# Where the causal mask enters a row of scores, and in what order a pair of heads is worked

## The chip, the cores and the metric

One core of one Trainium2 chip runs the whole kernel. The metric is device time in microseconds of one execution, lower is better.

## The reference

Two sequences of 1024 tokens, width 256, pass through one layer, all in float32.

1. Layer norm of x; q, k, v for 16 heads of 128 (`einsum('ihd,bpd->biph')`); scores q·k; where a key comes after its query the score is replaced by -1e10; softmax of scores / sqrt(128); the weighted sum of v; the output projection W_O; the result is added to x.
2. Layer norm again, then a mixture of 32 experts (8 chosen for each token, by groups) plus a shared expert; the result is added.

The change touches step 1 alone.

## The kernel before

**The work of a pair.** Attention is done for 8 pairs of heads of sequence 0, then 8 of sequence 1: 16 pairs, p = 0 to 15. In the code `a` is the head within a pair, `c` the half of the queries (512 each), and k = 2a + c. Every float32 value is split into a high and a low part, and each product is three matmuls (`three`). A pair is a list of steps, named by kind, k and n:

- `Rk.n`: one row of scores, 128 queries against all keys up to their own: (r+1)·128 wide, r from 0 to 7, in `ps_s[r % 2]`. TensorE does the matmuls, VectorE the row maximum (L1237), ScalarE the exponential into `prob` (L1055). R0 is the rows r = 4 to 7 of head 0, R1 the rows 0 to 3 of head 1, R2 the rows 4 to 7 of head 1, R3 the rows 0 to 3 of head 0 of the next pair.
- `Tk.n`: up to four 128x128 transposes of `prob` into `ps_t` (L783, one bank of two), the high part copied by ScalarE to `pT_hi` (L1071), the low part by VectorE (L1252). There are three `pT` buffers, used in turn.
- `Vk.n`: the product of that transposed block with v, added up in `ps_z`. The last V of a k is followed by `z_hi` on ScalarE and `z_lo` on VectorE.
- `Wk.n`: half of the output projection, into a `ps_t` bank (T and W take the two banks in turn), then two adds to `acc` on VectorE (L1267).
- `X0` to `X11`: projections (q, k, then v) through the one bank `ps_x`: matmuls, a ScalarE copy of the high part, a VectorE subtraction for the low part.

**The order.** TensorE, ScalarE and VectorE each walk the same list in the same order, each doing its own share of every step, and each runs in order: a wait of one step holds all that stands behind it on that engine. `PAIR` serves pairs 0 to 6 and 11 to 14 as it stands, and pairs 9 and 10 with routing steps of VectorE woven in evenly (`SLOTS`, `DISPATCH`). Pairs 7, 8 and 15 have lists of their own (`MIDDLE`, `ROUTE`, `LAST`).

**The waits of the steps.**

- R (TensorE): the exponential of the row two before in the sequence of R steps, since `ps_s` has two buffers.
- T (TensorE): all four exponentials of its block, and VectorE's last read of its `ps_t` bank, that is, of the step two before it among the T and W steps.
- T (ScalarE): the V step of the block three before it, since that block lies in the same `pT` buffer:

```
act.wait_ge(s_bank, p * BANKED + m + 1)
act.wait_ge(s_pv, p * TRS + t + PV0 - 2)
```

Here t counts the T steps of the pair (T0.n is n, T1.n is 4 + n, T2.n is 12 + n, T3.n is 16 + n), V steps are counted in the same way, `PV0` is 3 and `TRS` is 24. So T step t waits for V step t - 3.

- V (TensorE): VectorE's low part of its T step. W: `z_lo`. X: VectorE's low part of the X step before.

Of the kernel before, what the change touches and what calls it, by code (L numbers as in the profile page):

```python
# [12 lines left out]
P = 128  # L13
# [20 lines left out]


PAIR = """
T0.0 T0.1 R0.0 X0 T0.2 V0.0 T0.3 V0.1 R0.1 X1 V0.2 V0.3 R0.2 R0.3 W0.0 W0.1 X2 T1.0 T1.1 R1.0
R1.1 X3 T1.2 V1.0 T1.3 R1.2 V1.1 T1.4 V1.2 V1.3 T1.5 R1.3 V1.4 T1.6 T1.7 X4 V1.5 T2.0 V1.6 T2.1
V1.7 X5 T2.2 R2.0 W1.0 R2.1 W1.1 V2.0 V2.1 V2.2 T2.3 X6 V2.3 R2.2 R2.3 W2.0 W2.1 X7 T3.0 T3.1
R3.0 R3.1 X8 V3.0 T3.2 V3.1 T3.3 X9 T3.4 V3.2 T3.5 V3.3 T3.6 V3.4 T3.7 R3.2 V3.5 V3.6 V3.7 X10  # L40
R3.3 W3.0 W3.1 X11
"""


# [201 lines left out]
def width(r):  # L246

    return P * (r + 1)
# [7 lines left out]
def build(nc, ctx, x, w_a, w_b, w_o, router, bias, experts, out):  # L256
    def sb(name, shape, dt=F32, until=ctx):
        return until.enter_context(nc.sbuf_tensor(name, shape, dt))
# [12 lines left out]
    ident, ident_bf = sb("ident", [P, P]), sb("ident_bf", [P, P], BF16)  # L271
    causal = sb("causal", [P, P], BF16)
# [46 lines left out]
    with ExitStack() as attention:  # L319
# [11 lines left out]
        k_lo = [sb(f"k_lo{a}", [P, S], F32R, attention) for a in range(2)]  # L331
# [71 lines left out]
    EXP0, BANK0, PV0, X0, O0 = 2, 2, 3, 1, 1  # L403
# [313 lines left out]
    def _(pe):  # L717
        pe.sem_inc(s_pv, PV0)
        pe.wait_ge(s_const, 8)

        def three(to, w_hi, w_lo, m_hi, m_lo, start, stop):

            pe.matmul(to, w_hi, m_hi, start=start, stop=False)  # L723
            pe.matmul(to, w_hi, m_lo, start=False, stop=False)  # L724
            return pe.matmul(to, w_lo, m_hi, start=False, stop=stop)  # L725

        def transpose_xn(q, d, bank):

# [6 lines left out]
        def project(b, n, bank, weights):  # L735

            a, what, part = PROJ[n]
            if a == 1:
                pe.wait_ge(s_b, weights)
                w_hi, w_lo = b_hi, b_lo  # L740
            else:
                pe.wait_ge(s_a, weights)
                w_hi, w_lo = a_hi, a_lo
            if what == "v":
                for j in range(2):
                    t = b * S + (2 * part + j) * P
                    for d in range(ND):
                        m = slice(512 + d * 2 * DH, 512 + (d + 1) * 2 * DH)
                        last = three(bank[:, j * 2 * DH:(j + 1) * 2 * DH],
                                     xT_hi[:, d, t:t + P], xT_lo[:, d, t:t + P],  # L750
                                     w_hi[:, m], w_lo[:, m], d == 0, d == ND - 1)
            else:
                at = 0 if what == "q" else ND * DH
                t = b * S + part * NQ
                for d in range(ND):
                    w = slice(at + d * DH, at + (d + 1) * DH)
                    last = three(bank[:, :], w_hi[:, w], w_lo[:, w], xT_hi[:, d, t:t + NQ],
                                 xT_lo[:, d, t:t + NQ], d == 0, d == ND - 1)
            last.then_inc(s_x, 1)

        def scores(a, r, row, x_need):


            pe.wait_ge(s_exp, row + EXP0 - 1)
            pe.wait_ge(s_x_free, x_need + X0)
            q = slice(r * P, (r + 1) * P)
            to = ps_s[r % 2]
            for k0 in range(0, width(r), NQ):
                k1 = max(min(width(r), k0 + NQ), k0 + 2 * P)
                diagonal = k0 <= r * P < k1  # L770
                last = three(to[:, k0:k1], q_hi[a][:, q], q_lo[a][:, q], k_hi[a][:, k0:k1],
                             k_lo[a][:, k0:k1], True, not diagonal)
                if diagonal:
                    last = pe.matmul(to[:, r * P:(r + 1) * P], ident_bf[:, :], causal[:, :],  # L774
                                     start=False, stop=True)
            last.then_inc(s_scores, 1)

        def transpose(c, n, bank, use, rows):
# [31 lines left out]
        def attend(kind, k, n, m, p, order, x_before):  # L810

            a, c = k // 2, k % 2
            if kind == "R":
                na, c_, is_next = scored(k)
                r = c_ * BC + n
                scores(na, r, (p + 1) * ROWS + r if is_next else p * ROWS + na * NT + r,


                       x_before - 2 if k == 0 else
                       x_before + count_of(order, ("X", 2 * k - 1, 0)) + 1)  # L820
            elif kind == "T":
                transpose(c, n, ps_t[m % 2], p * BANKED + m, p * ROWS + a * NT + (c + 1) * BC)
            elif kind == "V":
                if a == 1 and n == 0:
                    pe.wait_ge(s_v1, p + 1)
                times_v(a, c, n, m, p * BANKED + count_of(order, ("T", k, n)))
            elif kind == "W":
                project_out(a, n, ps_t[m % 2], p * BANKED + m, p * 4 + k + 1,
                            p + 1 if a == 0 else p + 1 + O0)
# [146 lines left out]
        for kind, k, n, m in walk(START):  # L976
            bank = [ps_x, ps_z][(m or 0) % 2]
            if kind in "XY" and m >= 2:
                pe.wait_ge(s_x_free, X0 + m - 1)
            if kind == "Y":  # L980
                transpose_xn(k, n, bank)
            elif kind == "X":

                half = 1 if PROJ[k][1] != "v" and PROJ[k][2] == 1 or k >= X_OWN + 6 else 0
                pe.wait_ge(s_x_free, X0 + count_of(START, ("Y", half, ND - 1)) + 1)
                project(0, k, bank, 1 if k < X_OWN + 4 else 2)
            elif kind == "R":
                scores(0, n, n, count_of(START, ("X", X_OWN + 1, 0)) + 1)
# [600 lines left out]
```

## Time and profile before

| | us |
|---|---|
| median of 3 runs | 1553.6 |
| lowest and highest | 1549.8, 1571.86 |
| the profiled execution | 1570.57 |
| its span, first to last instruction | 1568.8 |

The trace is of the profiled execution. In rows of stretches the columns are: the stretch and its length in us, then busy us and instructions (x) of TensorE's matmuls (PE), its weight loads (PEld), VectorE (DVE), ScalarE (ACT) and GpSimd (POOL), TensorE's granted clock as a share of 2.4 GHz, the DMA share and GB/s. In timeline rows they are: start, duration, engine, line, operation, what it writes and reads, and in brackets the idle time before it with what ended it; x7 means that seven neighbours are merged. Its times of single instructions are compared within that execution; between an instruction's start and the next one's start on TensorE lies what it really costs there, because matmuls overlap and their ends are modelled.

### The profile page before, as it was taken

How to read it: one execution, taken by the hardware profiler on the slowest of the kernel's cores; microseconds unless marked ns; L12 is line 12 of the kernel's file. 1: busy time of each engine (PE TensorE's matmuls, PEld its weight loads, DVE VectorE, ACT ScalarE, POOL GpSimd, SP SyncE). 2: the span in 40 equal slices, each digit the busy share in tenths (PEclk: the TensorE clock that was granted, in tenths of full speed). 3: DMA queues.
4: the chain of work that ended last, by engine and by line, in shares of the span. 5: the costliest groups of instructions: out<-in, count | busy, mean ns of one | idle time of the engine just before them, and what ended most of it. 6: DMA issues, size and time to landing. Idle time of an engine off the chain costs nothing.

```text
span 1568.8 us, 29528 instructions
## 1 busy us (share of the span) xinstructions
PE 1361.8 (87%) x8752; PEld 1183.9 (75%) x8752; DVE 963.8 (61%) x2021; ACT 717.3 (46%) x1662; POOL 601.1 (38%) x571
## 2 busy tenths in 40 slices
PE   5999999999998799999999999988863985598891
PEld 4888888888886678777888888877753884487781
DVE  5666666666678586878666666668541431365455
ACT  2555555555554444444555555533431541344330
POOL 4642642642616223031553643100554005354326
PEclk9999999999998999999999999999995998799896
DMA  3356356356343600000211202034874867699733
GB/s 112 118 191 228 111 197 226 106 198 231 104 164 132 204 14 18 11 24 5 75 47 40 74 20 104 3 126 162 311 258 155 279 212 258 191 384 336 248 106 111
DMA packets 132601, 231.16 MB, mean 147 GB/s; under 512 B 9632, under 2 KB 103840, under 8 KB 132512
## 3 DMA queue, kind: packets, MB, share of 16 engines
q1 hardware_dynamic: 69104, 145.16, 27.3%
q10 hardware_dynamic: 51120, 51.26, 10.0%
q0 software_dynamic: 12288, 33.57, 6.2%
q8 instruction: 54, 0.88, 0.2%
q14 instruction: 35, 0.29, 0.1%
HBM read 121.42 MB, written 108.53 MB: 147 GB/s over the span
## 4 chain that ended last, share of the span: by engine, by line
PE 63%; DVE 10%; issue 6%; another core or an unknown queue 6%; DMA 6%; ACT 3%; POOL 3%; SPq 1%; ACTq 0%; POOLq 0%; DVEq 0%
PE ps_s L723 7%; PE ps_t L783 6%; PE ps_s L725 6%; PE ps_s L724 6%; PE ps_z L723 5%; PE ps_x L723 5%; PE ps_x L724 5%; PE ps_x L725 5%; PE ps_z L725 4%; PE ps_z L724 4%; PE ps_t L723 3%; PE ps_t L724 2%; PE ps_t L725 2%; PE ps_s L918 2%
## 5 line engine op out<-in xcount | busy, mean ns | idle before, releaser
L1055 ACT ACTIVATE prob<-ps_s,neg_max 128x128 f32<-128x128 f32 (+7 forms) x256 | 189.6, 742 | 300.9 <-DVE neg_max L1237 288.4
L1252 DVE TENSOR_TENSOR pT_lo<-ps_t,pT_hi 128x512 fp32r<-128x512 f32 (+2 forms) x320 | 191.4, 602 | 65.6 <-ACT pT_hi L1071 62.5
L1237 DVE TENSOR_REDUCE neg_max<-ps_s 128x1 f32<-128x128 f32 (+7 forms) x256 | 188.9, 750 | 10.5 <-PE ps_s L774 8.7
L783 PE MATMUL ps_t<-ident,prob 128*128 128x128 f32 x1152 | 180.5, 275 | 14.8 <-DVE pT_lo L1252 10.6
L1071 ACT ACTIVATE pT_hi<-ps_t 128x512 fp32r<-128x512 f32 (+2 forms) x320 | 165.0, 535 | 49.9 <-PE ps_t L783 46.3
L623 POOL DMA_INDIRECT xs<-xn,slots x128 | 125.2, 978 | 143.8 <-DVE slots L1394 56.9
L783 PEld LDWEIGHTS ps_t<-ident,prob 128*128 128x128 f32 x1152 | 141.0, 142 | 49.3 <-DVE pT_lo L1252 16.8
L723 PE MATMUL ps_s<-k_hi,q_hi 128*128 128x512 f32 (+2 forms) x384 | 148.6, 387 | 0.7 <-DVE k_lo L1232 0.4
L723 PE MATMUL ps_s<-ring,a_hi 128*128 x384 | 125.0, 325 | 23.9 <-issue 17.1
L550 POOL TENSOR_TENSOR a_hi<-raw_a,zero 128x512 fp32r<-128x512 f32 x32 | 33.4, 1043 | 292.6 <-PE ps_x L725 239.3
L1465 DVE TENSOR_TENSOR a_lo<-ps_s,a_hi 128x512 fp32r<-128x512 f32 x96 | 66.3, 690 | 122.9 <-ACT a_hi L1122 92.5
L690 POOL DMA_INDIRECT yg<-ys,slots x64 | 65.6, 1024 | 190.8 <-DMA ys<-yq 101.7
L725 PE MATMUL ps_s<-k_hi,q_lo 128*128 128x512 f32 (+2 forms) x384 | 133.3, 347 | 0.0
L724 PE MATMUL ps_s<-k_lo,q_hi 128*128 128x512 f32 (+2 forms) x384 | 133.2, 347 | 0.0
L723 PE MATMUL ps_z<-pT_hi,v_hi 128*128 128x512 f32 (+2 forms) x320 | 131.7, 412 | 1.0 <-DVE pT_lo L1252 1.0
L1099 ACT ACTIVATE sg<-ps_s 128x256 f32<-128x256 f32 x112 | 43.2, 386 | 194.6 <-PE ps_s L725 118.1
L1449 DVE TENSOR_TENSOR h<-sg,ps_s 128x256 f32<-128x256 f32 x112 | 46.9, 419 | 128.0 <-ACT sg L1099 100.0
L724 PE MATMUL ps_s<-ring,a_hi 128*128 x384 | 115.3, 300 | 2.7 <-issue 2.6
L725 PE MATMUL ps_z<-pT_hi,v_lo 128*128 128x512 f32 (+2 forms) x320 | 115.9, 362 | 0.0
L724 PE MATMUL ps_z<-pT_lo,v_hi 128*128 128x512 f32 (+2 forms) x320 | 115.4, 361 | 0.0
L725 PE MATMUL ps_s<-ring,a_lo 128*128 x384 | 112.3, 292 | 0.0
L723 PEld LDWEIGHTS ps_s<-ring,a_hi 128*128 128x128 f32 x384 | 77.8, 203 | 42.0 <-issue 41.1
(265 smaller groups left out, 3933.2 us busy)
## 6 DMA issues: line engine op xcount, KB each, us to landing
ring<-ws SPq DMA_DIRECT2D x60, 768.0 KB
ws<-split_to SPq DMA_DIRECT2D x34, 768.0 KB, 4.1
xs<-taken SPq DMA_DIRECT2D x16, 1536.0 KB, 9.8
xq<-xs ACTq DMA_DIRECT2D x48, 512.0 KB
ys<-yq ACTq DMA_DIRECT2D x48, 512.0 KB
raw<-experts_dram SPq DMA_DIRECT2D x34, 384.0 KB, 4.6
ys<-taken SPq DMA_DIRECT2D x8, 1536.0 KB, 14.6
raw_a<-w_a_dram SPq DMA_DIRECT2D x15, 512.0 KB, 10.5
```

The costliest lines, as they stand in the source:

```text
L623: pool.indirect_dma_start(xs[b], bass.IndirectOffsetOnAxis(ap=slots[b][:, t, k:k + 1], axis=0), xn[:, t, :], None).then_inc(s_xs[b][i % le ...
L690: pool.indirect_dma_start(yg[n], None, ys[b], bass.IndirectOffsetOnAxis(ap=slots[b][:, t, k:k + 1], axis=0)).then_inc(s_yg[n], 16)
L723: pe.matmul(to, w_hi, m_hi, start=start, stop=False)
L724: pe.matmul(to, w_hi, m_lo, start=False, stop=False)
L725: return pe.matmul(to, w_lo, m_hi, start=False, stop=stop)
L783: last = pe.transpose(bank[:, j * P:(j + 1) * P], prob[c][:, j, n * P:(n + 1) * P], ident[:, :])
L1055: act.activation(prob[c][:, j, 0:width(r)], ps_s[r % 2][:, 0:width(r)], ACT.Exp, bias=neg_max[:, r:r + 1], accum_out=row_sum[:, c, j:j + 1 ...
L1071: act.activation(to, ps_t[m % 2][:, j * P:], ACT.Copy).then_inc(s_hi, 1)
L1237: dve.tensor_reduce(neg_max[:, r:r + 1], ps_s[r % 2][:, 0:width(r)], AX.X, ALU.max, negate=True).then_inc(s_max, 1)
L1252: dve.tensor_tensor(lo, ps_t[m % 2][:, j * P:], hi.bitcast(F32), ALU.subtract).then_inc(s_bank_free, 1)
L1449: dve.tensor_tensor(by[0], by[1], ps_gu[g % 2].rearrange("p (j m i) -> p j m i", j=2, m=2)[:, :, 1], ALU.mult).then_inc(s_h, 1)
L1465: dve.tensor_tensor(xs_lo[g % 2], ps_xT[u % 2], xs_hi[g % 2].bitcast(F32), ALU.subtract).then_inc(s_xs_lo, 1)
```

## The change

Two things. In `scores`, the matmul that lays the mask (identity, stationary, by `causal`, 128x128 in bf16) moves from the end of a row to its start and opens the accumulation of the bank; the three products of the diagonal chunk are then added onto it (`start` false), with the group check switched off. And `PAIR` lists the same steps in another order. No step is added or left out.

```
--- before.py
+++ after.py
@@ -34,11 +34,10 @@
 
 
 PAIR = """
-T0.0 T0.1 R0.0 X0 T0.2 V0.0 T0.3 V0.1 R0.1 X1 V0.2 V0.3 R0.2 R0.3 W0.0 W0.1 X2 T1.0 T1.1 R1.0
-R1.1 X3 T1.2 V1.0 T1.3 R1.2 V1.1 T1.4 V1.2 V1.3 T1.5 R1.3 V1.4 T1.6 T1.7 X4 V1.5 T2.0 V1.6 T2.1
-V1.7 X5 T2.2 R2.0 W1.0 R2.1 W1.1 V2.0 V2.1 V2.2 T2.3 X6 V2.3 R2.2 R2.3 W2.0 W2.1 X7 T3.0 T3.1
-R3.0 R3.1 X8 V3.0 T3.2 V3.1 T3.3 X9 T3.4 V3.2 T3.5 V3.3 T3.6 V3.4 T3.7 R3.2 V3.5 V3.6 V3.7 X10
-R3.3 W3.0 W3.1 X11
+T0.0 R0.0 R0.1 T0.1 T0.2 V0.0 X0 R0.2 R0.3 V0.1 V0.2 T0.3 X1 T1.0 T1.1 V0.3 X2 T1.2 R1.0 R1.1 W0.0
+X3 T1.3 R1.2 W0.1 R1.3 V1.0 V1.1 T1.4 T1.5 X4 V1.2 V1.3 T1.6 T1.7 R2.0 R2.1 V1.4 V1.5 T2.0 T2.1 V1.6
+X5 V1.7 T2.2 R2.2 R2.3 W1.0 W1.1 X6 V2.0 T2.3 T3.0 V2.1 V2.2 V2.3 T3.1 T3.2 X7 R3.0 W2.0 W2.1 V3.0
+V3.1 T3.3 X8 V3.2 T3.4 T3.5 R3.1 X9 V3.3 V3.4 T3.6 T3.7 R3.2 V3.5 V3.6 V3.7 X10 R3.3 W3.0 W3.1 X11
 """
 
 
@@ -718,11 +717,11 @@
         pe.sem_inc(s_pv, PV0)
         pe.wait_ge(s_const, 8)
 
-        def three(to, w_hi, w_lo, m_hi, m_lo, start, stop):
-
-            pe.matmul(to, w_hi, m_hi, start=start, stop=False)
-            pe.matmul(to, w_hi, m_lo, start=False, stop=False)
-            return pe.matmul(to, w_lo, m_hi, start=False, stop=stop)
+        def three(to, w_hi, w_lo, m_hi, m_lo, start, stop, joins=False):
+
+            pe.matmul(to, w_hi, m_hi, start=start, stop=False, skip_group_check=joins)
+            pe.matmul(to, w_hi, m_lo, start=False, stop=False, skip_group_check=joins)
+            return pe.matmul(to, w_lo, m_hi, start=False, stop=stop, skip_group_check=joins)
 
         def transpose_xn(q, d, bank):
 
@@ -765,14 +764,13 @@
             pe.wait_ge(s_x_free, x_need + X0)
             q = slice(r * P, (r + 1) * P)
             to = ps_s[r % 2]
+            pe.matmul(to[:, r * P:(r + 1) * P], ident_bf[:, :], causal[:, :], start=True, stop=False,
+                      skip_group_check=True)
             for k0 in range(0, width(r), NQ):
                 k1 = max(min(width(r), k0 + NQ), k0 + 2 * P)
                 diagonal = k0 <= r * P < k1
                 last = three(to[:, k0:k1], q_hi[a][:, q], q_lo[a][:, q], k_hi[a][:, k0:k1],
-                             k_lo[a][:, k0:k1], True, not diagonal)
-                if diagonal:
-                    last = pe.matmul(to[:, r * P:(r + 1) * P], ident_bf[:, :], causal[:, :],
-                                     start=False, stop=True)
+                             k_lo[a][:, k0:k1], not diagonal, True, diagonal)
             last.then_inc(s_scores, 1)
 
         def transpose(c, n, bank, use, rows):
```

## Rows read from the trace of the kernel before

**Rows 1.** The page: busy us of each engine, share of the span, instructions.

```profile
PE 1361.8 (87%) x8752; PEld 1183.9 (75%) x8752; DVE 963.8 (61%) x2021; ACT 717.3 (46%) x1662; POOL 601.1 (38%) x571
```

**Rows 2.** Busy time by stretch: a plain pair, the two woven pairs (9, 10), a later plain pair.

```profile
155.00:214.00 59.00, 59.00 (x377) 51.14 (x377) 39.48 (x77) 32.44 (x76) 27.02 (x20) 1.00 0.53 177
...
605.00:670.00 65.00, 61.03 (x379) 51.38 (x378) 50.83 (x132) 32.14 (x77) 13.92 (x12) 1.00 0.06 17
670.00:740.00 70.00, 63.20 (x387) 52.33 (x387) 59.29 (x112) 32.16 (x77) 14.71 (x12) 1.00 0.06 16
...
800.00:860.00 60.00, 58.98 (x375) 50.93 (x375) 39.15 (x76) 32.36 (x76) 29.35 (x28) 1.00 0.15 52
```

**Rows 3.** Timeline, TensorE: the seven transposes that open four of the pairs.

```profile
155.90 0.93 PE L783 MATMUL ps_t<-ident,prob 128*128 128x128 f32 x7
...
215.00 0.93 PE L783 MATMUL ps_t<-ident,prob 128*128 128x128 f32 x7
...
860.80 0.93 PE L783 MATMUL ps_t<-ident,prob 128*128 128x128 f32 x7
...
921.22 0.93 PE L783 MATMUL ps_t<-ident,prob 128*128 128x128 f32 x7
```

**Rows 4.** Waits of TensorE, 605 to 740 us; then 740 to 981 us: total, times, longest.

```profile
PE ps_t L783 <- ACT prob L1055: 3.4, 3, 1.7
...
PE ps_x L723 <- DVE q_lo L1227: 4.1, 4, 1.1
```

**Rows 5.** VectorE groups by shape, 158 to 451 us: busy, mean ns, idle before.

```profile
L1252 DVE TENSOR_TENSOR pT_lo<-ps_t,pT_hi 128x512 fp32r<-128x512 f32 x59 | 40.2, 683 | 12.6 <-ACT pT_hi L1071 12.0
L1267 DVE SCALAR_TENSOR_TENSOR acc<-ps_t,inv_sum,acc 128x256 f32<-128x256 f32 x80 | 33.4, 475 | 0.0
...
L1237 DVE TENSOR_REDUCE neg_max<-ps_s 128x1 f32<-128x1024 f32 x10 | 12.2, 1224 | 2.1 <-PE ps_s L774 2.1
```

**Rows 6.** ScalarE groups by shape, the same stretch.

```profile
L1071 ACT ACTIVATE pT_hi<-ps_t 128x512 fp32r<-128x512 f32 x59 | 34.3, 599 | 6.8 <-PE ps_t L783 6.2
...
L1055 ACT ACTIVATE prob<-ps_s,neg_max 128x768 f32<-128x768 f32 x10 | 9.0, 903 | 14.6 <-DVE neg_max L1237 14.6
```

**Rows 7.** Timeline from the end of row R2.3 to T3.0 of one pair.

```profile
312.61 0.39 PE L724 MATMUL ps_s<-k_lo,q_hi 128*128 128x512 f32 x1
...
312.84 0.40 PE L725 MATMUL ps_s<-k_hi,q_lo 128*128 128x512 f32 x1
313.07 0.10 PEld L774 LDWEIGHTS ps_s<-causal,ident_bf 128*128 128x128 bf16 x1 [0.27 <-issue]
313.08 0.23 PE L774 MATMUL ps_s<-causal,ident_bf 128*128 128x128 bf16 x1
...
313.12 0.36 PE L723 MATMUL ps_t<-o_hi,z_hi 128*128 128x256 f32 x1
...
313.32 0.28 PE L724 MATMUL ps_t<-o_lo,z_hi 128*128 128x256 f32 x1
...
313.35 1.23 DVE L1237 TENSOR_REDUCE neg_max<-ps_s 128x1 f32<-128x1024 f32 x1 [0.24 <-PE ps_s L774]
...
313.44 0.28 PE L725 MATMUL ps_t<-o_hi,z_lo 128*128 128x256 f32 x1
...
314.61 1.12 ACT L1055 ACTIVATE prob<-ps_s,neg_max 128x1024 f32<-128x1024 f32 x1 [0.36 <-DVE neg_max L1237]
...
315.62 0.19 ACT L1055 ACTIVATION_READ_ACCUMULATOR prob<-ps_s,neg_max 128x1 f32 x1
...
315.86 0.98 PEld L783 LDWEIGHTS ps_t<-ident,prob 128*128 128x128 f32 x8
316.04 1.04 PE L783 MATMUL ps_t<-ident,prob 128*128 128x128 f32 x8
```

**Rows 8.** Timeline, TensorE: the first matmuls after one stall.

```profile
829.03 0.50 PE L723 MATMUL ps_x<-xT_hi,a_hi 128*128 128x512 f32 x1 [1.02 <-DVE q_lo L1227]
829.37 0.39 PE L724 MATMUL ps_x<-xT_lo,a_hi 128*128 128x512 f32 x1
```

## The prediction

> **What bounds the kernel now.** I read the page first, for how full each engine is: TensorE is busy 87% of the span, VectorE 61%, ScalarE 46% [rows 1]. An average hides stages, so next come the stretches. In a plain pair TensorE is busy 59.00 of 59.00 us at clock 1.00, with 39.5 us on VectorE and 32.4 on ScalarE [rows 2]. The openings of two such pairs are 59.10 us apart, of two late ones 60.42 [rows 3]. Where does TensorE wait? In pairs 1 to 6 the view of waits lists nothing; in pairs 9 and 10 it lists several, the largest 3.4 us for exponentials; in pairs 11 to 14, 4.1 us in four waits [rows 4]. So where the changed list rules, TensorE's own work is the bound, and two questions remain: does that work get cheaper, and are its waits still covered?
>
> **The price list of TensorE** is the step from one start to the next: 0.23 us for a 512-wide matmul (312.61 to 312.84) and 0.12 for a 256-wide one (313.32 to 313.44), 0.109 for a transpose (eight in 1.04 us less the last one's 0.27, over seven steps: 0.11) [rows 7]. For 384 wide I take three quarters of 512, 0.175, an estimate. A block of four transposes is 0.44, a full V 0.70, a q or k projection 1.39, a W step 0.71. With 0.13 for each mask the steps of a pair add up to 59.07 us, the measured 59.10: nothing is left over to be gained in a plain pair by order alone.
>
> **The mask.** It starts at 313.08; the next matmul starts at 313.12 but takes until 313.32, 0.20 instead of 0.12. The mask thus costs 0.04 + 0.08 and 0.01 in front, 0.13 us. Its weight load starts at 313.07, when the product ahead has streamed, not at that product's start as the others do [rows 7]. At the head of a row it again stands between other matmuls and costs the same 0.13. Only where a transpose stands before it could it be cheaper, which no row shows: T then R occurs 7 times in the new list. Bounds: nothing saved, and 0.064 us saved if the transpose streams only half of its 0.109; a transpose's step looks like full streaming, so I take 0.008, 91 times in 13 pairs, 0.7 us (0 to 5.8). The accumulation itself costs nothing more. The Trainium skill (PSUM — Partial Sum Buffer, on `first_mm` and the zero region) says the opening matmul clears the flags of the whole bank, so that later products add where the mask lies and overwrite elsewhere; no row here shows that, and it is why no second opener is needed. The same notes (TensorE: Matmul & The Clock Gate, Back-to-back issue gap and Weight-path perf modes) give 56 ns for a 128-column matmul and a fast load for weights that aren't FP32, which would make a mask behind transposes 0.07 us cheaper, 6.6 us in all; the trace's 0.13 speaks against it where a product stands ahead.
>
> **The order, and which waits lose their cover.** A hand-over is read off the one chain in full view: last product at 312.84, mask 313.08, maximum 313.35 for 1.23 us, exponential 314.61 for 1.12, its sum read until 315.81, TensorE's load for T3.0 at 315.86, its transposes at 316.04 [rows 7]. So a row's data are gone 2.7 us after TensorE leaves it, and the old list gives that wait 2.8: full, but by 0.2 us only. With the mask first, the last product ends the row, and its end comes 0.20 after TensorE's turn to the next step. A T block takes 0.20 + 0.60 on ScalarE + 0.03 + 0.69 on VectorE + 0.04 = 1.56 us before its bank is free [rows 5, 6]. Each engine in order, I then walked the new list, with TensorE's steps above, and VectorE's and ScalarE's shapes from their groups. T step t may be copied only after V step t - 3. The old list always has that V ahead of the T. The new list breaks this five times: T1.3 before V1.0, T1.5 before V1.2, T1.7 before V1.4, T2.1 before V1.6, T3.0 before V2.1. The copy then stands at the head of ScalarE's queue, with the exponentials behind it, and on VectorE the row maxima and the adds of W behind its low part. What becomes late on TensorE:
>
> 1. T1.0 wants the exponential of R0.3. Between lie V0.1, V0.2, T0.3 and X1, 2.38 us, where 2.70 are needed: 0.32. X2 then waits 0.08 for X1's low part.
> 2. T1.4 wants the bank of T1.3, copied after V1.0. Between V1.0 and T1.4 stands V1.1 alone, 0.70 against 1.56: 0.86.
> 3. T1.5 wants the bank of W0.1, whose adds (0.86 a pair, two of 475 ns less their overlap) stand on VectorE behind T1.3 and a 384-wide maximum: 0.71 more.
> 4. T1.7 wants the bank of T1.5, copied after V1.2: V1.3 and T1.6 give 0.92, needed with a 384-wide block are 1.31: 0.39.
> 5. T2.2 wants the bank of T2.0. Behind V1.4 there follow one after the other T1.7's copy and low part, the maxima of R2.0 and R2.1, the second exponential (0.90), then T2.0's copy and low part: 4.70 us. TensorE has V1.5, T2.0, T2.1, V1.6, X5 and V1.7, 3.39: 1.31.
> 6. T3.2 wants the bank of T3.0, copied after V2.1: V2.2, V2.3 and T3.1 are 1.16 against 1.56: 0.40.
>
> Together 4.08 us a pair. After a stall the first weight load isn't hidden either: the first matmul at 829.03 steps to the second in 0.34 us where 0.23 is usual [rows 8]. Seven stalls add 0.7. A plain pair becomes 59.1 + 4.8 = 63.9 us. All later steps (R3.1, X9, V3.3 to X11) keep over 0.3 us, and the end of the list is the same.
>
> **The sum.** Eleven plain pairs (0 to 6, 11 to 14): +52.8. The wait that pairs 11 to 14 have now, 1.02 us before X5 [rows 4], has V1.2 to V1.6 as cover in the new list: -4.1; if that cover doesn't work, 0. Pairs 9 and 10 have VectorE busy 59 of 70 us in the fuller one [rows 2], and wait by what is woven in; the same chains lengthen, by nothing more than now if VectorE sets the pace anyway, by 8 us a pair if each woven step falls into a chain. I take +5 each, near the plain pair's 4.8, +10. Mask: -0.7. SyncE's and GpSimd's loads and splits hang on steps that move by at most a few us in a pair where their buffers are idle for longer; taken as 0, at worst 1 us a pair. The sum is +58.0 us: 1570.6 would become 1628.6 in an execution like the profiled one. That one lies 17 us over the median; I add to the median: 1553.6 + 58.0 = 1611.6 us.
>
> **The rivals.**
>
> - *The order is neutral (0.12).* The waits are covered by slack I don't see, and a pair stays at 59.1, its sum of steps. For it: the sum fits, and there is no idle time before. Against it: the same hand-over arithmetic puts T3.0 of the old list 0.2 us from waiting, and its load is in fact released at 315.86 just before its turn. Time: 1553.6 - 0.7 = 1553.
> - *Half the price (0.08).* ScalarE's copies overlap, or a stall early in the pair covers the later ones: 2.2 us a pair in 13 pairs, 1582.
> - *Faster (0.03).* One mechanism: the new order takes the waits out of pairs 9 to 14, where TensorE stands idle for 4.0 + 6.8 and 4.1 us [rows 2, 4], and a mask behind transposes saves its 5.8. Time: 1553.6 - 15 - 6 = 1533. It decides only if no T copy waits for its V, that is, if the five inversions come free.
> - *The clock falls too (0.07).* The pairs would be idle 7% of their time, in pieces. The fuller woven pair is idle 6.8 of 70 us at clock 1.00 [rows 2], which speaks against it. If a tenth of 800 us ran at the lower of the two levels (1.2 instead of 2.4 GHz), some 40 us more: 1650.
>
> **How the numbers follow.** My forecast has 0.70. Its own bounds: without the unhidden loads, with nothing in pairs 9 and 10 and the full mask gain, 11 x 4.1 - 4.1 - 5.8 = +35, 1589; with 8 in each woven pair, no cover for the old wait and 1 us more a pair for loads, 52.8 + 16 + 11 = +80, 1633. An execution like the slowest of the three would add 18 to the likely value, 1630. The range is 1586 to 1640, and leaves out the neutral case, the faster one and the falling clock. This measurement tells 2%, 31 us, from no change. Slower by more than that: the forecast, the clock, and half of the half price, 0.81. Faster by over 2% would need under 1523: 0.01. The rest is within 2%.
>
> **What would show it.** Openings of plain pairs near 63.9 us apart instead of 59.1; TensorE waiting in every plain pair on `ps_t` transposes released by `pT_lo` and by the adds to `acc`, the longest near 1.3 us before T2.2; ScalarE's `pT_hi` released by `ps_z` matmuls, which it isn't now; the mask's weight load at the head of each row, the step still 0.13. Openings 59 us apart would prove the walk wrong; waits in place but longer than the sum would mean that I mis-sized a chain, T1.5's and T2.2's first.

## The result and the profile after

The changed kernel took 1605.29 us in the median (1595.66 to 1613.28, 4 runs), the kernel before 1553.24 beside it: ratio 1.0302, interval 1.0256 to 1.0348. Slower, by 52 us, where 58 more were forecast. Some executions of either kernel fall into a slower state, as the profiled one of the kernel before did (1570.57 us); all ratios here are of fast executions alone, and so need not be the quotient of two medians.

The page of the changed kernel, busy us of each engine, against [rows 1]:

```profile
span 1602.2 us, 29550 instructions
...
PE 1373.7 (86%) x8752; PEld 1190.4 (74%) x8752; DVE 964.9 (60%) x2021; ACT 720.3 (45%) x1662; POOL 602.9 (38%) x571
```

Every engine has the same number of instructions as before, and nearly the same busy time. A page alone would not say where 52 us went. The timeline of TensorE does, with the transposes that open four pairs, against [rows 3]:

```profile
163.21 0.60 PE L781 MATMUL ps_t<-ident,prob 128*128 128x128 f32 x4
...
226.87 0.60 PE L781 MATMUL ps_t<-ident,prob 128*128 128x128 f32 x4
...
902.23 0.60 PE L781 MATMUL ps_t<-ident,prob 128*128 128x128 f32 x4
...
965.90 0.60 PE L781 MATMUL ps_t<-ident,prob 128*128 128x128 f32 x4
```

A plain pair now takes 63.66 us, early and late ones alike; before it was 59.10 and 60.42. The stretches, against [rows 2] (same columns):

```profile
164.00:227.00 63.00, 59.90 (x373) 51.42 (x372) 39.57 (x76) 32.03 (x75) 26.97 (x20) 1.00 0.49 165
...
640.00:705.00 65.00, 58.45 (x366) 49.77 (x366) 48.72 (x130) 30.19 (x71) 10.75 (x11) 1.00 0.05 15
705.00:775.00 70.00, 60.96 (x354) 51.47 (x353) 57.14 (x105) 30.75 (x73) 11.80 (x10) 0.95 0.05 16
```

TensorE, never idle in a plain pair before, is idle for 3.1 of 63 us, at full clock. Its waits in pairs 2 to 6, a view that listed nothing before (total, times, longest):

```profile
PE ps_t L781 <- DVE pT_lo L1250: 11.8, 20, 1.1
PE ps_t L781 <- DVE acc L1265: 3.0, 5, 0.6
```

In each pair four transposes wait for a low part and one for the adds to `acc`, all for the bank that they write. A sixth, before T1.0, leaves only 0.14 us idle, too little for that view; the timeline has it at TensorE's weight load, released by an exponential:

```profile
174.21 0.91 PEld L781 LDWEIGHTS ps_t<-ident,prob 128*128 128x128 f32 x8 [0.58 <-ACT prob L1053]
```

Who holds VectorE? ScalarE's waits in the same stretch:

```profile
ACT pT_hi L1069 <- PE ps_z L724: 20.7, 15, 2.7
...
ACT pL_hi L1069 <- PE ps_z L724: 15.9, 5, 3.2
```

ScalarE's copies of transposed blocks wait for matmuls into `ps_z`, which are V steps. The kernel before had no such row. These are four holds a pair: T1.3 (2.70 us), T1.5 (0.83), T1.7 (3.19) and T3.0 (0.61). The fifth inversion, T2.1 before V1.6, holds nothing: its copy comes some 2 us after V1.6 for other reasons. One such chain in full, from the timeline:

```profile
193.75 0.34 PE L722 MATMUL ps_z<-pT_hi,v_hi 128*128 128x384 f32 x1
...
193.95 0.28 ACT L1069 ACTIVATE pL_hi<-ps_t 128x128 fp32r<-128x128 f32 x1 [3.19 <-PE ps_z L724]
...
194.26 0.29 DVE L1250 TENSOR_TENSOR pL_lo<-ps_t,pL_hi 128x128 fp32r<-128x128 f32 x1 [2.84 <-ACT pL_hi L1069]
...
194.47 1.68 DVE L1235 TENSOR_REDUCE neg_max<-ps_s 128x1 f32<-128x640 f32 x2
...
195.32 0.80 ACT L1053 ACTIVATE prob<-ps_s,neg_max 128x640 f32<-128x640 f32 x1 [1.09 <-DVE neg_max L1235]
...
196.18 0.90 ACT L1053 ACTIVATE prob<-ps_s,neg_max 128x768 f32<-128x768 f32 x1
...
197.07 0.97 ACT L1069 ACTIVATE pT_hi<-ps_t 128x512 fp32r<-128x512 f32 x2
...
197.69 0.69 DVE L1250 TENSOR_TENSOR pT_lo<-ps_t,pT_hi 128x512 fp32r<-128x512 f32 x1 [1.54 <-ACT pT_hi L1069]
...
198.44 0.44 PE L781 MATMUL ps_t<-ident,prob 128*128 128x128 f32 x2 [1.13 <-DVE pT_lo L1250]
```

V1.5 starts at 193.75, so V1.4 is done; at 193.95 T1.7's copy starts after ScalarE has idled 3.19 us in front of it. Then low part, two maxima, two exponentials, T2.0's copy and its low part follow one another, and T2.2 starts at 198.44, 1.13 us after TensorE had nothing more to do. It is item 5 of the prediction, step for step.

### The profile page after: what moved, and what is told of

It is laid out like the page before. It is cut to its first block, busy times and chain, and to the rows that moved or that the text cites. A ratio compares the mean times of both kernels' runs of the same rounds, so it can differ in the third digit from the quotient of the medians.

```text
span 1602.2 us, 29550 instructions
## 1 busy us (share of the span) xinstructions
PE 1373.7 (86%) x8752; PEld 1190.4 (74%) x8752; DVE 964.9 (60%) x2021; ACT 720.3 (45%) x1662; POOL 602.9 (38%) x571
## 4 chain that ended last, share of the span: by engine, by line
PE 35%; issue 15%; DMA 15%; POOL 13%; DVE 9%; SPq 5%; another core or an unknown queue 4%; ACT 4%; POOLq 0%; ACTq 0%; DVEq 0%
DMA raw_a<-w_a_dram 6%; PE ps_s L722 5%; SPq L462 4%; PE ps_s L723 4%; PE ps_s L724 4%; PE ps_t L781 3%; POOL split_to L552 3%; POOL split_to L549 3%; DMA raw_b<-w_b_dram 3%; PE ps_z L722 2%; PE ps_x L722 2%; DMA raw_o<-w_o_dram 2%; DMA ring<-ws 2%; PE ps_x L723 2%
## 5 line engine op out<-in xcount | busy, mean ns | idle before, releaser
L781 PEld LDWEIGHTS ps_t<-ident,prob 128*128 128x128 f32 x1152 | 136.2, 142 | 98.6 <-DVE pT_lo L1250 57.8
L722 PE MATMUL ps_s<-k_hi,q_hi 128*128 128x512 f32 (+2 forms) x384 | 155.7, 405 | 0.0
L722 PE MATMUL ps_z<-pT_hi,v_hi 128*128 128x512 f32 (+2 forms) x320 | 121.5, 380 | 0.0
L1265 DVE SCALAR_TENSOR_TENSOR acc<-ps_t,inv_sum,acc 128x256 f32<-128x256 f32 x256 | 107.2, 474 | 0.2 <-PE ps_t L724 0.2
```

Source lines behind the costliest of these rows:

```text
L722: pe.matmul(to, w_hi, m_hi, start=start, stop=False, skip_group_check=joins)
L781: last = pe.transpose(bank[:, j * P:(j + 1) * P], prob[c][:, j, n * P:(n + 1) * P], ident[:, :])
L1265: last = dve.scalar_tensor_tensor(to, ps_t[m % 2][:, j * D:(j + 1) * D], inv_sum[:, c, q:q + 1], to, ALU.mult, ALU.add)
```

## The experiments

The runs e1 to e4 fell on one chip, e5 to e7 on a second and e8 to e11 on a third, on which the kernel before itself takes 1565.6, 1474.8 and 1475.8 us in the median; so each run is compared with the kernel before on its own chip, and plain pairs are compared by their length, which in pairs 1 to 6 is the same on all chips to 0.1 us, for the kernel before (59.10 and 59.11) as for the changed one (63.64 twice). Pair lengths in the table are means between the ends of VectorE's adds of W in successive pairs 1 to 6; idle is that of TensorE in one of them. By their times alone e3 lies within 2% of before and e4 (1.0082 to 1.0218) is unclear; what is read from them is read from the pairs.

| run | median us | ratio to before, interval | plain pair | idle |
|---|---|---|---|---|
| e1, mask first, list of before | 1565.09 | 0.9992 (0.9951 to 1.0033) | 58.95 | 0 |
| e2, new list, mask last | 1617.81 | 1.0304 (1.0227 to 1.0380) | 63.7 | 3.06 |
| e3, five T behind their V | 1576.33 | 1.0087 (1.0056 to 1.0118) | 60.8 | 0.92 |
| e4, diagonal's wait relaxed | 1590.28 | 1.0150 (1.0082 to 1.0218) | 62.3 | 1.97 |
| e5, T1.3 alone moved back | 1526.41 | 1.0362 (1.0343 to 1.0380) | 63.0 | 2.64 |
| e6, an inversion put into before | 1475.96 | 1.0001 (0.9986 to 1.0015) | 59.1 | 0 |
| e7, a list meant to be better | 1475.54 | 1.0011 (0.9997 to 1.0024) | 59.0 | 0 |
| e8, before again, one execution | 1475.0 | | 59.1 | 0 |
| e9, the changed kernel again | 1533.43 | 1.0392 (1.0376 to 1.0408) | 63.65 | 3.10 |
| e10, e7's list in plain pairs only | 1475.86 | 0.9999 (0.9987 to 1.0011) | 58.97 | 0 |
| e11, V1.0 moved up | 1511.10 | 1.0237 (1.0222 to 1.0252) | 61.9 | 1.79 |

**The two parts apart.** e1 has the changed `scores` with the list of before, e2 the reverse.

> The list of before, the mask as the opening matmul. Waits theory (the new list puts transposes ahead of the V step whose buffer they need): plain pairs stay at 59.1 us, no waits of TensorE in pairs 1 to 6; a mask behind a transpose costs 0.11 instead of 0.13 us, as in the changed kernel's trace, so some 112 rows save 2 us in all: 1551. Rival, the mask is the cause (products added onto an opened bank are slower, or a row is ready later): the 52 us come back here, plain pairs near 63.6 us, 1605.

> The list of the changed kernel, the mask as the closing matmul. Waits theory: the same six waits in each plain pair, each within 0.1 us of the changed kernel's, pairs 63.7 us, 1606 in all. Rival, the mask is the cause: 1553. If the two parts need each other, neither kernel alone shows the 52 us.

The order alone brings the whole loss (1.0304 against the changed kernel's 1.0302), with the same waits; the mask alone brings none. The mask's place is out as a cause.

The mask's own price shows in the changed kernel's timeline. Behind a matmul product, and behind a transpose:

```profile
164.69 0.28 PE L724 MATMUL ps_s<-k_hi,q_lo 128*128 128x256 f32 x1
164.82 0.23 PE L767 MATMUL ps_s<-causal,ident_bf 128*128 128x128 bf16 x1
164.86 0.48 PE L722 MATMUL ps_s<-k_hi,q_hi 128*128 128x512 f32 x1
165.18 0.39 PE L723 MATMUL ps_s<-k_lo,q_hi 128*128 128x512 f32 x1
...
181.03 0.22 PE L767 MATMUL ps_s<-causal,ident_bf 128*128 128x128 bf16 x1
181.06 0.42 PE L722 MATMUL ps_s<-k_hi,q_hi 128*128 128x384 f32 x1
181.32 0.34 PE L723 MATMUL ps_s<-k_lo,q_hi 128*128 128x384 f32 x1
181.49 0.34 PE L724 MATMUL ps_s<-k_hi,q_lo 128*128 128x384 f32 x1
```

Behind a product it is 0.04 to the next start and 0.09 of that one's stretch (0.32 for 0.23), 0.13 as before. Behind a transpose it is 0.03 + 0.09 (0.26 for the 0.17 of the last step), with nothing lost in front: 0.11 to 0.12. With seven rows of a pair behind transposes that is the 0.1 to 0.15 us by which e1's pairs are shorter, 2 us in the kernel, too little for its time to show.

**All five inversions out.** e3 changes the new list only by moving T steps:

```
-X3 T1.3 R1.2 W0.1 R1.3 V1.0 V1.1 T1.4 T1.5 X4 V1.2 V1.3 T1.6 T1.7 R2.0 R2.1 V1.4 V1.5 T2.0 T2.1 V1.6
+X3 R1.2 W0.1 R1.3 V1.0 T1.3 V1.1 T1.4 X4 V1.2 T1.5 V1.3 T1.6 R2.0 R2.1 V1.4 T1.7 V1.5 T2.0 V1.6 T2.1
...
-V2.0 T2.3 T3.0 V2.1
+V2.0 T2.3 V2.1 T3.0
```

> The changed kernel with five transposes moved behind the V step that they wait for (T1.3, T1.5, T1.7, T2.1, T3.0). Waits theory, by the same walk: the waits before T1.4, T1.5, T1.7 and T2.2 go; 0.3 before T1.0 and 0.4 before T3.2 stay, since those blocks stand too near their banks anyway; T1.7 now stands behind the exponentials of R2.0 and R2.1, and T2.1 waits 0.6 for its bank. With 0.1 after each wait a plain pair takes 60.7 us, 1569 in all. Rival, the new list is slow for another reason (its grouping of steps, rows of scores in twos): pairs stay above 63, 1600 or more.

60.8 us a pair where 60.7 were worked out, and three waits of the kind foretold (0.14 us idle before T1.0, 0.44 before T2.1, released by `pL_lo`, 0.34 before T3.2). So 2.8 of the 4.55 us a pair are gone with five moved steps, and the rival falls. The other 1.7 us need no inversion: they are blocks that stand too near the exponential or the bank they want, T1.0 in the new list as it is, T2.1 and T3.2 in e3's.

**One wait relaxed, with no step moved.** The diagonal blocks (T0.3, T1.7, T2.3, T3.7) lie in a buffer of their own, and need not wait for V step t - 3. Only T1.7 stands ahead of that V:

```
-                act.wait_ge(s_pv, p * TRS + t + PV0 - 2)
-                j = max(n - c * BC, 0)
+                j = max(n - c * BC, 0)
+                if j < BC - 1:
+                    act.wait_ge(s_pv, p * TRS + t + PV0 - 2)
+                else:
+                    before = {0: 0, 1: 4, 2: 12, 3: 16}[k]
+                    act.wait_ge(s_pv, p * TRS + before + PV0)
```

> The changed kernel, with one wait of ScalarE relaxed: the diagonal block of each k, which has a buffer of its own, now waits for the last reader of that buffer instead of for V step t - 3. Only T1.7 is freed by it. Waits theory: the wait before T2.2 (1.13 us idle in the trace) goes, the five others stay; 1.2 to 1.4 us a plain pair, pairs 62.4, some 17 us in all, 1588. Rival, T2.2 is late because two exponentials and a projection stand before it anyway: nothing moves, 1605.

The pair falls by 1.35 us, and the wait before T2.2 is the one that is gone; the other five stand at 0.14, 0.72, 0.59, 0.26 and 0.27 us idle. This is the cleanest proof of item 5: the list is that of the changed kernel, only the wait of ScalarE differs.

**One inversion at a time: a miss, and its repair.** e5 moves T1.3 behind V1.0.

```
-X3 T1.3 R1.2 W0.1 R1.3 V1.0 V1.1 T1.4 T1.5
+X3 R1.2 W0.1 R1.3 V1.0 T1.3 V1.1 T1.4 T1.5
```

> The changed kernel with T1.3 alone moved back behind V1.0. Waits theory: the waits before T1.4 (0.72 us idle in the trace of the changed kernel) and before T1.5 (0.59, released by the adds to acc, which stand behind T1.3's low part) go together, those before T1.0, T1.7, T2.2 and T3.2 stay; with 0.27 of each wait hidden under the modelled end of the matmul ahead, 1.85 us a plain pair: 61.8 instead of 63.65, some 22 us in all. Rival, the wait before T1.5 has its own cause, the place of W0.1: only the first goes, 1.0 us a pair, 62.7.

61.8 us were expected and 63.0 measured. Moving T1.3 back put W0.1 ahead of it, and so swapped the turns of the two `ps_t` banks: T1.5 now wants the bank of T1.3, not that of W0.1. From the timeline of e5:

```profile
185.30 1.35 DVE L1250 TENSOR_TENSOR pT_lo<-ps_t,pT_hi 128x512 fp32r<-128x512 f32 x2 [1.33 <-ACT pT_hi L1069]
186.04 0.55 PE L781 MATMUL ps_t<-ident,prob 128*128 128x128 f32 x3 [0.83 <-DVE pT_lo L1250]
```

A wait of 0.83 us has come in the place of 0.72 and 0.59. So I moved the V instead of the T, which keeps the turns:

```
-X3 T1.3 R1.2 W0.1 R1.3 V1.0 V1.1 T1.4 T1.5
+X3 V1.0 T1.3 R1.2 W0.1 R1.3 V1.1 T1.4 T1.5
```

> The changed kernel with V1.0 moved up, ahead of T1.3, R1.2, W0.1 and R1.3. Unlike e5 this leaves the turns of the two ps_t banks as they are (in e5 T1.5 got the bank of T1.3 instead of that of W0.1, which gave it a new wait of 0.84 us). Waits theory: the waits before T1.4 (0.72) and T1.5 (0.59) both go, the other four stay: 61.8 us a plain pair. Rival, the wait before T1.5 is W0.1's own: 62.7.

61.9 us a pair. The waits of TensorE in e11, of which 14 in this stretch (four pairs and a half), none is released by `acc` any more; e9, the changed kernel on the same chip, has both rows. First e11, then e9:

```profile
PE ps_t L781 <- DVE pT_lo L1250: 8.0, 14, 1.1
```

```profile
PE ps_t L781 <- DVE pT_lo L1250: 10.2, 17, 1.1
PE ps_t L781 <- DVE acc L1265: 3.0, 5, 0.6
```

So the wait before T1.5 was T1.3's too, passed on through VectorE's queue, as item 3 had it.

**An inversion with room behind it.** e6 moves T1.3 ahead of V1.0 in the list of before.

```
-T1.2 V1.0 T1.3 R1.2 V1.1 T1.4
+T1.2 T1.3 V1.0 R1.2 V1.1 T1.4
```

> The kernel before with one inversion put in: T1.3 moved ahead of V1.0, so that ScalarE's copy of T1.3 waits for V1.0 with the exponential of R1.2 behind it. Waits theory: an inversion costs only where the next user of the bank stands nearer than 1.56 us behind the V; here T1.5, the next user, stands 2.5 us behind V1.0, so pairs stay at 59.1 and the time is that of before. Rival, each inversion costs by itself (ScalarE held is TensorE held): 0.9 us a plain pair, 10 us in all.

Nothing: 59.1 us a pair, no wait, 1.0001. But the test was weak. The timeline of e6 has the last product of V1.0 and the copies of T1.2 and T1.3:

```profile
172.98 1.31 ACT L1070 ACTIVATE pT_hi<-ps_t 128x512 fp32r<-128x512 f32 x2
...
173.26 0.40 PE L724 MATMUL ps_z<-pT_hi,v_lo 128*128 128x512 f32 x1
```

Two copies of 0.60 us span 1.31: T1.2's copy ended just before V1.0 did, and T1.3's was held for 0.1 us. So e6 shows that an inversion costs nothing where it hardly holds ScalarE, as T2.1's shows in the changed kernel; whether a long hold is free too, with room behind it, was not tested. That each inversion costs the same by itself is ruled out by the other runs: relaxing T1.7's wait gave 1.35 us (e4), and taking T1.3's inversion out 0.65 (e5) or 1.75 (e11). The price of 1.56 us of hand-over less the work that stands between the V and the next user of the bank rests on the waits of the changed kernel (the table further down).

**A better version.** The kernel before had one wait left in plain pairs, [rows 4], before X5. e7 takes the mask from the change and moves R2.0 and T2.2:

```
-V1.7 X5 T2.2 R2.0 W1.0 R2.1
+V1.7 R2.0 T2.2 X5 W1.0 R2.1
```

> The kernel before with the mask opening the row, and R2.0 and T2.2 moved between V1.7 and X5, so that X4's low part has 3.4 us instead of 2.0 before X5 needs its bank. No transpose is ahead of its V. Waits theory: pairs 1 to 6 take 58.9 us as with the mask alone; pairs 11 to 14 lose their one wait before X5 and fall from 60.3 to 59.0; 5 us less from these four and 2 from the mask, 7 us under before (0.995). Rival: X4's copy is late by itself in these pairs and delays W1.0 or T2.2's bank instead, nothing gained beyond the mask's 2 us.

No gain. Two things were found. Pairs 11 to 14 had no wait on this chip to begin with; and pairs 9 and 10, where routing steps stand in VectorE's queue, took 66.7 and 71.2 us instead of 65.2 and 69.8 in e6. In e10, which has the mask first but keeps the old list there, they take 65.2 and 69.7, so it is the moved list that costs this. The reason may be that R2.0's maximum now stands ahead of others; that wasn't tested. Three more runs:

> The kernel before, unchanged, for its profile on the chip of this call. All theories: plain pairs 1 to 6 at 59.1 us without a wait. In pairs 11 to 14 the wait of 1 us before X5 either stands (then it belongs to the kernel) or is absent (then to the chip: e6 and e7 ran on another chip than the runs before them, and have none there).

> The moved R2.0 and T2.2 of e7 in the plain pairs alone; pairs 9 and 10 keep the list of before, which was 1.4 us a pair faster there. Waits theory: the 2 us of the mask and nothing lost, attention 2 to 3 us shorter than before's on a chip where pairs 11 to 14 have no wait (0.998, hardly to be told by times), 7 us on one where they have (0.9955). Rival: the mask's saving is lost in other pairs: 1.000.

> The changed kernel, unchanged, on the chip of this call. Waits theory: six waits in each plain pair, 63.65 us a pair, the same to 0.1 us on any chip; attention ends 48 us later than in the kernel before where that has its wait in pairs 11 to 14, 53 later where it hasn't.

e8, the kernel before unchanged, has no wait in pairs 11 to 14 either (59.1 us). That wait appeared in the first profile of the kernel before and in e1, on the slower chip, and on neither of the faster ones: ScalarE starts the copy of X4 1.6 us after its input's last matmul ended (825.31 against 823.67), where in e6 it starts 0.04 us after. e1's timeline has it, released by nothing that the profile names:

```profile
825.31 0.60 ACT L1045 ACTIVATE q_hi<-ps_x 128x512 fp32r<-128x512 f32 x1 [1.81 <-remote]
```

e10 keeps the old list in pairs 9 and 10, and its attention ends at 1028.9 us against e8's 1030.9, the 2 us of the mask. The whole time is 0.9999 of before's, from 0.9987 to 1.0011: 2 us of 1475 can't be told. Whether e10 gains the further 5 us on a chip that has the wait wasn't tried. No version here beats the kernel before by more than the measurement tells.

e9 shows the change at its full price, where the old wait isn't there to be saved: 57.6 us, 1.0392. The wait of pairs 11 to 14 had given 5 us of it back in the first comparison. Its attention ends 56.5 us after e8's, where 53 were expected; 2.2 of the 3.5 lie in pair 0, which ends 5.0 us later than e8's, where the first two profiles had 2.8 between them.

## Why the prediction was right

**The mechanism** (the walk of the new list, V step t - 3 before the copy of T step t). Shown by e2, e3, e4 and e11: the order alone makes the loss, putting V first or relaxing one wait takes out its share and no more. No run took out the waits of items 1 and 6; they stand where the walk put them, with the releasers that it named.

**The sizes.** TensorE's idle time before a transpose is counted from the modelled end of the matmul ahead. That end lies 0.16 us behind the turn of the next step (0.39 or 0.40 for a step of 0.23), and the first block after a wait is 0.06 longer (0.66 for 0.60). So idle + 0.22 is the loss:

| wait before | forecast, with 0.10 for the load | idle, after | loss |
|---|---|---|---|
| T1.0 | 0.42 | 0.14 | 0.36 |
| X2 | 0.18 | none shown | 0.15 |
| T1.4 | 0.96 | 0.72 | 0.94 |
| T1.5 | 0.81 | 0.59 | 0.81 |
| T1.7 | 0.49 | 0.26 | 0.48 |
| T2.2 | 1.41 | 1.13 | 1.35 |
| T3.2 | 0.50 | 0.26 | 0.48 |

X2's wait shows as no idle time, since the modelled end of the matmul ahead covers it. From the timeline of the changed kernel, with the transposes of T1.0 and T1.1 first:

```profile
174.22 1.15 PE L781 MATMUL ps_t<-ident,prob 128*128 128x128 f32 x8
...
174.85 0.69 DVE L1230 TENSOR_TENSOR k_lo<-ps_x,k_hi 128x512 fp32r<-128x512 f32 x1 [0.20 <-ACT k_hi L1047]
...
175.44 0.28 PE L724 MATMUL ps_z<-pL_hi,v_lo 128*128 128x256 f32 x1
...
175.59 0.50 PE L722 MATMUL ps_x<-xT_hi,b_hi 128*128 128x512 f32 x1
...
175.94 0.40 PE L723 MATMUL ps_x<-xT_lo,b_hi 128*128 128x512 f32 x1
```

X1's low part ends at 175.54 and X2 starts at 175.59, 0.15 us after the matmul ahead instead of 0.12, and takes 0.35 to its second matmul instead of 0.23: 0.15 us lost. The eight transposes take 1.15 us where eight take 1.04 [rows 7], 0.05 more than the 0.06 after a wait: T1.1 was held as well, by T0.3's low part, which ends at 174.65 where T1.1's weight load starts at 174.71; no item had that.

The losses come to 4.57 us, with T1.1's 4.62, and 0.13 less for the mask, where the pair grew by 4.55: less than 0.1 stays unaccounted for. The forecast was 4.8. Each of its seven waits came where it was put, with the releaser that it named, and within 0.06 us. What was sized too high is the load after a wait: 0.10, read off a 512-wide matmul, where before transposes it is 0.06.

**The terms of the sum.** Eleven plain pairs at +4.8, 52.8: measured 4.55 each in pairs 1 to 6, and on e9's chip 32 us in pairs 0 to 6 and 18 in 11 to 14, 50. The old wait before X5, -4.1: it was 1.3 us a pair in the lengths, -5.2, in the first profile, and 0 on two other chips; I had taken something that seems to come with the chip for a trait of the kernel. So e9's 57.6 us lie near the forecast's 58.0 by luck: on that chip this term is 0, and the same sum would give 62. Pairs 9 and 10, +10: measured +3.0 and +4.5 (end to end 65.3 to 68.3 and 69.8 to 74.3). The mask, -0.7: 2 at most. At the end of the last pair the two first profiles differ by 48 us: 30.0 from pairs 0 to 6, -2.4 from pairs 7 and 8, whose lists are unchanged, 7.5 from pairs 9 and 10, and 12.7 from pairs 11 to 14. The forecast had 33.6, 0, 10 and 15.1 for these, less 0.7: every group was put some 2 to 4 us too high. The medians differ by 52, inside the range; where the other 4 us arise was not looked into.

**The rivals.** Neutral and faster fell with the first comparison; half the price too: no copy overlapped and no early wait covered a later one. The falling clock didn't come in the plain pairs, which show 1.00 with 3.1 us idle in 63. It came in the fuller woven pair alone: 0.95, where TensorE idles 9.0 of 70 us (0.98 in e9), against 1.00 in the kernel before. What that cost is within the 4.5 us by which that pair grew.

**The weight of the pages.** The 56 ns that the Trainium skill (TensorE: Matmul & The Clock Gate, Back-to-back issue gap) gives for the isolated gap of a 128-column matmul, from which the prediction estimated 6.6 us, isn't what the trace shows: 0.11 to 0.12 us behind transposes, 0.13 elsewhere, 2 us in all at most.

## What to carry to other kernels

Where several engines walk one written-out order, check each move against the waits of the engines that don't bound the kernel: a wait placed ahead of its producer holds everything queued behind it, and costs TensorE, where the hold is long, the hand-over time less the work that stands between. Before trusting a new order, list for each ring of buffers which step must precede which, and what the move does to the turns of every shared bank; and walk it with durations of the trace, which here gave each of seven waits to 0.06 us. A wait whose cause the profile doesn't name may come with the chip: look for it on another one before spending a change on it.

## What was not expected

The same kernel takes 1475 us on two chips and 1566 on another (1553 in the first comparison), and nearly all of the difference lies behind the attention. The stretch from there on, first the kernel before as first profiled, then e8 (columns as in [rows 2]):

```profile
1040.00:1540.00 500.00, 375.96 (x2615) 339.73 (x2615) 232.31 (x549) 185.69 (x423) 172.30 (x175) 0.89 0.68 233
```

```profile
1034.00:1473.00 439.00, 363.30 (x2624) 326.80 (x2623) 244.27 (x575) 186.45 (x424) 193.88 (x193) 0.94 0.77 273
```

TensorE has the same work in both; on the faster chip the DMA moves 273 GB/s instead of 233, and the granted clock is 0.94 instead of 0.89. The kernel moves the same bytes on both, so the higher rate may be the cause of the shorter time or only another way to state it; that memory traffic sets the pace of that stage on the slower chip wasn't tested. At the end of the attention the two profiles differ by 6.8 us, of which the late copy in pairs 11 to 14 makes 5.2; its cause stays open.
